# A gated cross-attention and ternary FFN block on one core: gate factor apart, last down product in column halves, weight rounding on GpSimd without the wait on VectorE

## What is computed

```python
qp = ctx @ Wq.T + bq;  kp = ctx @ Wk.T + bk
scores = (qp @ kp.T) * 128 ** -0.5 * layernorm(x)      # 512 x 512 for each of 4 batches
p = softmax(where(mask, -inf, scores))
x = x + tanh(g_xattn) * p

def quant_weight(w):                                   # ternary weights
    scale = mean(abs(w)) + EPS
    return clip(round(w / scale), -1, 1), scale
def quant_act(x):                                      # 8-bit rows
    s = max(abs(x), axis=-1) / 127 + EPS
    return clip(round(x / s), -128, 127), s
def qlinear(x, w): wq, ws = quant_weight(w); xq, xs = quant_act(x); return xq @ wq.T * xs * ws

h = layernorm(x)
x = x + tanh(g_ffn) * qlinear(silu(qlinear(h, w_gate)) * qlinear(h, w_up), w_down)
```

## Time and profile before

| | us |
|---|---|
| median of 3 runs | 224.27 (223.83 to 224.95) |
| the profiled execution | 224.45 |
| its span in the trace | 222.5 |
| TensorE busy in the span | 199.3 |
| VectorE busy | 180.2 |
| ScalarE busy | 124.5 |
| GpSimd busy | 97.8 |

### The profile page before, as it was taken

The page is one execution under the profiler, slowest core; times in us unless marked ns, Lnnn a source line. Parts: engine busy times, 40 slices in busy tenths (PEclk is TensorE's granted clock), DMA queues, the critical chain, the costliest instruction groups (busy, mean ns, idle before and its releaser), DMA issues.

```text
span 222.5 us, 2846 instructions
## 1 busy us (share of the span) xinstructions
PE 199.3 (90%) x854; PEld 90.3 (41%) x854; DVE 180.2 (81%) x359; ACT 124.5 (56%) x165; POOL 97.8 (44%) x154
## 2 busy tenths in 40 slices
PE   8764008999999998999999999999999999999994
PEld 7221004344444344444444444444444444444441
DVE  0598979799989799797997989888898987888721
...
PEclk9995555899999999999999999999999999999999
...
GB/s 215 420 423 423 417 391 424 281 325 8 3 47 47 115 186 172 98 0 3 47 64 121 153 91 15 69 80 74 141 3 175 201 89 13 96 79 16 97 188 94
DMA packets 47360, 32.84 MB, mean 148 GB/s; under 512 B 40944, under 2 KB 41072, under 8 KB 45808
## 3 DMA queue, kind: packets, MB, share of 16 engines
...
## 4 chain that ended last, share of the span: by engine, by line
PE 71%; DMA 14%; ACT 5%; DVE 4%; issue 2%; SPq 2%; DVEq 0%
PE pU L947 23%; PE pG L934 23%; PE pD L965 20%; DMA stage_b<-in_L_ffn_w_up 8%; DMA stage_a<-in_L_ffn_w_down 4%; PE pA L909 3%; ACT down_w L689 2%; DMA stage_b<-stage_b 2%; ACT L736 1%; ACT hid L736 1%; DVE abs_part L1345 1%; SPq L351 1%; PE pA L898 1%; ACT stage_b L743 1%; DVE am L1320 1%
## 5 line engine op out<-in xcount | busy, mean ns | idle before, releaser
L736 ACT ACTIVATE hid<-pG,act_g 128x512 f32<-128x512 f32 x64 | 43.6, 688 | 54.6 <-PE pG L934 54.4
L934 PE MATMUL pG<-gate_w,xqT 128*128 128x512 f16 x256 | 64.7, 388 | 1.4 <-DVE xqT L1303 0.8
L947 PE MATMUL pU<-up_w,xqT 128*128 128x512 f16 x256 | 62.7, 379 | 0.0
L965 PE MATMUL pD<-down_w,stage_b 128*128 128x512 f16 x256 | 57.3, 379 | 0.6 <-DMA stage_b<-stage_b 0.6
L1311 DVE TENSOR_TENSOR hid<-pU,hid 128x512 f32<-128x512 f32 x64 | 43.6, 685 | 11.1 <-PE pU L947 9.2
L934 PEld LDWEIGHTS pG<-gate_w,xqT 128*128 128x128 f16 x256 | 25.1, 100 | 37.0 <-issue 8.0
L965 PEld LDWEIGHTS pD<-down_w,stage_b 128*128 128x128 f16 x256 | 24.9, 98 | 31.8 <-issue 2.3
L947 PEld LDWEIGHTS pU<-up_w,xqT 128*128 128x128 f16 x256 | 25.1, 98 | 31.3 <-issue 1.7
L743 ACT ACTIVATE stage_b<-hid,inv 128x1024 f16<-128x1024 f32 x15 | 16.9, 1139 | 7.8 <-DVE inv L1329 7.8
L560 POOL TENSOR_SCALAR out_scale<-den,act_e,down_k 128x1 f32<-128x1 f32 x16 | 5.9, 371 | 33.4 <-DVE den L1326 33.4
L909 PE MATMUL pA<-kT,qT 128*128 128x512 f32 x26 | 15.4, 678 | 4.9 <-ACT kT L709 4.9
...
## 6 DMA issues: line engine op xcount, KB each, us to landing
...
out<-x SPq DMA_DIRECT2D x8, 256.0 KB, 2.4
out<-stage_b SPq DMA_DIRECT2D x8, 256.0 KB, 2.4
ctx_s<-in_ctx SPq DMA_DIRECT2D x4, 256.0 KB, 14.4
...
```

The lines of the kernel that those rows point to most:

```text
L736: act.activation(hid[:, t % NH, n * 512:(n + 1) * 512], pG[c % NG][:, :], ACT.Silu, scale=act_g[:, t:t + 1]).then_inc(silu_done, 1)
L934: ins = pe.matmul(pG[c % NG][:, :], xqT[:, t // TILES % 2, t % TILES, k, :], gate_w[:, n, k, :], start=k == 0, stop=k == KD - 1)
L947: ins = pe.matmul(pU[c % NU][:, :], xqT[:, t // TILES % 2, t % TILES, k, :], up_w[:, n, k, :], start=k == 0, stop=k == KD - 1)
L965: ins = pe.matmul(pD[t % ND][:, :], hidT[:, t % 2, k, :], down_w[:, k // KD, k % KD, :], start=k == 0, stop=k == KI - 1)
```

## The change

Four things, and a new order of all engines' lists around them.

- The factor `rsum * tanh_g` becomes one VectorE instruction per group of tiles (`rgate[:, t0:t1]`). Where GpSimd adds the residual, the multiplication of `probs` by it is a call of its own, `gate_probs(t)`, on ScalarE (9 tiles: 4, 6 to 10, 12, 14, 15) or GpSimd (1, 5, 13). VectorE still does tiles 0, 2, 3 and 11 in one instruction.
- The down product of tile 15 is made in column halves: 16 matmuls of 256 columns into one `pD` bank, then 16 into the other, with a `residual2_columns` and a `store_columns` of 128 KB for each.
- GpSimd's `weight_round` no longer waits for the bound of the chunk ahead.
- `k_copy(1)` and `k_copy(2)` go to VectorE. In the tables `CENTRE_BY`, `QUANTISE_BY`, `HQ_BY`, `ABS_BY` and `SIGN_BY` other engines are named. Each of the five lists is in another order.

```diff
+        GATE_BY = "-P--APAAAAA-APAA"
-        ABS_BY = ["AAAV", "AVAA", "AAAA"]
-        SIGN_BY = ["QXXX", "QQQX", "XXQQ"]
+        ABS_BY = ["AAVA", "AAAA", "AAAA"]
+        SIGN_BY = ["XQXQ", "QQXQ", "QXQX"]
...
             def residual1(t):
-                probs_t = probs[:, t % NP, :]
-                pool.wait_ge(tanh_done, 1)
-                pool.wait_ge(rsum_done, group_of(t) + 1)
-                pool.tensor_scalar(probs_t, probs_t, rsum[:, t:t + 1], tanh_g[:, 0:1], ALU.mult, ALU.mult)\
-                    .then_inc(gated, 1)
-                pool.wait_ge(gated, upto(RESIDUAL_BY, t))
-                pool.tensor_tensor(xt(t), probs_t, xt(t), ALU.add).then_inc(x2_pool, 1)
+                who = GATE_BY[t]
+                pool.wait_ge({"A": gated_act, "P": gated_pool}[who], upto(GATE_BY, t))
+                pool.tensor_tensor(xt(t), probs[:, t % NP, :], xt(t), ALU.add).then_inc(x2_pool, 1)
...
                 pool.wait_ge(winv_done, m + 1)
-                if m or n:
-
-                    wait_ternary(pool, *divmod(NC * m + n - 1, NC))
...
+            def gate_probs(t):
+                probs_t = probs[:, t % NP, :]
+                act.wait_ge(rgate_ready, group_of(t) + 1)
+                act.activation(probs_t, probs_t, ACT.Identity, scale=rgate[:, t:t + 1]).then_inc(gated_act, 1)
...
+            def down_columns(t, half):
+
+                cols = slice(half * 256, half * 256 + 256)
+
+                bank = pD[(t + half) % ND]
+                pe.wait_ge(final_ready, t - ND + 1 + half)
+                for k in range(KI):
+                    if half == 0 and k % 8 == 0:
+                        pe.wait_ge(hidT_ready[t % 2][k // 8], 16 * (t // 2 + 1))
+                    ins = pe.matmul(bank[:, cols], hidT[:, t % 2, k, :], down_w[:, k // KD, k % KD, cols],
+                                    start=k == 0, stop=k == KI - 1)
+                ins.then_inc(down_half, 1)
...
+            def residual2_columns(t, half):
+                cols = slice(half * 256, half * 256 + 256)
+                dve.wait_ge(down_half, 2 * t + half + 1)
+                if half == 0:
+                    dve.wait_ge(oscale_ready, t + 1)
+                dve.scalar_tensor_tensor(xt(t)[:, cols], pD[(t + half) % ND][:, cols], out_scale[:, t:t + 1], xt(t)[:, cols],
+                                         ALU.mult, ALU.add).then_inc(final_ready, 1)
```

More of the change, by code:

```diff
@@ L584, in _ @@
             valid_sums(0)
+            exp_bias(1)
             mask(2)
[L586 removed]
+            gate_probs(1)
             residual1(1)
[L588 removed]
             valid_sums(1)
[L590 removed]
+            centre(0)
             std2(0)
+            gate_scales(0)
             quantise_x(0)
[L593 to L597 removed]
+            centre(2)
             std2(1)
[L599 to L600 removed]
+            weight_round(0, 1)
             quantise_x(2)
@@ L815, in _ @@
             silu(6, 0)
+            silu(6, 1)
+            quantise_hidden(4, 0)
+            silu(6, 2)
+            quantise_hidden(4, 1)
+            silu(6, 3)
+            silu(7, 0)
             exp(8)
@@ L819, in _ @@
             exp(11)
-            silu(6, 1)
-            quantise_hidden(4, 1)
-            silu(6, 2)
-            silu(6, 3)
             quantise_hidden(5, 1)
-            silu(7, 0)
             silu(7, 1)
-            centre(8)
+            gate_probs(8)
+            gate_probs(9)
+            gate_probs(10)
             quantise_hidden(6, 0)
+            quantise_hidden(6, 1)
+            centre(9)
             silu(7, 2)
@@ L1135, in _ @@
             gate(10, 3)
+            gate(11, 0)
             up(10, 3)
-            gate(11, 0)
             up(11, 0)
@@ L1464, in _ @@
+            product(3, 0)
+            absmax_hidden(2, 1)
+            weight_bound(2, 3)
+            absmax_x(4)
+            inverse_hidden(2)
+            stats2(5)
             product(3, 1)
-            inverse_hidden(2)
+            residual2(0)
             absmax_hidden(3, 0)
+            absmax_x(5)
             product(3, 2)
-            stats2(4)
+            inverse_x(2)
             product(3, 3)
-            residual2(0)
+            inverse_std2(2)
             absmax_hidden(3, 1)
-            absmax_x(4)
+            residual2(1)
@@ L1473, in _ @@
             inverse_hidden(3)
-            residual2(1)
-            stats2(5)
-            stats1(9)
             stats2(6)
-            absmax_x(5)
-            inverse_std2(2)
-            inverse_x(2)
+            reciprocal_scale(2)
+            stats2(7)
+            residual2(2)
             absmax_x(6)
-            residual2(2)
-            stats2(7)
+            inverse_std2(3)
+            absmax_x(7)
+            product(4, 0)
+            inverse_x(3)
+            product(4, 1)
             score(8)
-            reciprocal_scale(2)
@@ L1486, in _ @@
-            absmax_x(7)
+            absmax_hidden(4, 0)
             mask_and_max(8)
-            inverse_x(3)
+            residual2(3)
+            reciprocal_scale(3)
+            stats1(10)
             score(9)
-            residual2(3)
+            stats1(11)
             mask_and_max(9)
-            product(4, 0)
-            inverse_std2(3)
-            stats1(10)
-            product(4, 1)
+            stats1(12)
+            product(4, 2)
+            stats1(13)
+            product(4, 3)
@@ L1523, in _ @@
+            residual2(4)
+            product(6, 2)
+            gate_sums(3)
             product(6, 3)
+            absmax_hidden(6, 1)
+            product(7, 0)
+            inverse_hidden(6)
             stats2(8)
-            absmax_hidden(6, 1)
+            product(7, 1)
             stats2(9)
-            inverse_hidden(6)
-            residual2(4)
-            residual1(11)
             absmax_x(8)
-            product(7, 0)
+            residual2(5)
             absmax_x(9)
-            residual2(5)
@@ L1650, in _ @@
             residual2(14)
-            residual2(15)
+            residual2_columns(15, 0)
+            residual2_columns(15, 1)
 _TRANSPOSED = ("ctx_512", "L0_xattn_Wq", "L0_xattn_Wk", "L0_ffn_w_gate", "L0_ffn_w_up", "L0_ffn_w_down")
```

549 lines of the change are left out of this document (276 added, 273 removed).

## The result

The changed kernel takes **226.20 us** (median of 8 runs, 225.41 to 226.91), the kernel before 224.38 beside it: ratio **1.0078** (95%: 1.0065 to 1.0091), 1.8 us slower. The forecast of 223.5 and its sign were wrong; 226.2 is the last value of the range, and the case that came true is the second rival (226.0). The profiled execution took 226.07 us, its span is 224.3 us, against 224.45 and 222.5 before.

The account below looks back on a forecast made before the run. TensorE was taken as almost never idle from its first gate product, with VectorE and ScalarE having to keep up. 224.45 - 0.2 (front and middle) - 0.6 (end) = 223.65, or 223.5 against the 224.27 median; range 221.6 to 226.2.

Parts of the forecast that it names:

- the second rival: ScalarE's exponentials and table loads ahead of silu(1, 3) become the bound, 2.5 us more: 226.0; chance 0.22.
- What GpSimd gains by not waiting: GpSimd's weight_round without its wait: at most 4.8 us gained in one place, off TensorE's path, hidden.
- The walk through ScalarE's list: ScalarE's calls counted from 20.3 us with trace durations: last down chunk summed at 48.2, silu(1, 3) done at 62.7.
- TensorE's account: TensorE's work done by 62.7 us: new 22.9, old 23.8, so 0.9 behind; old then loses 1.3 us by 93.
- any slip of one engine: In ScalarE's exponential block before silu(1, 3), a slip passes to both other engines; 2.5 us more, 226.0; chance 0.22.
- Head start kept: Front: down chunks land 2.5 us apart, weight_sum(2) at 46.5, all behind it 1.7 us earlier: 221.8; chance 0.23.
- The end: Tile 15's column halves: 32 matmuls in 3.5 us, shorter residual and store; -0.6 us, bounds -0.8 and +0.9.
- The weight-load rival: Weight loads of the last down product's column halves show, 16 times 0.1 us: 225.1; chance 0.04.
- The gate factor: Behind 93 us, nine gate_probs on ScalarE, some 0.6 us each, lie beside down and up products.
- The signs of being wrong: Prediction wrong if TensorE has a new idle stretch behind 63 us, or the clock falls again between 35 and 48.

Follow-up runs that it names:

- a_old_wait: The changed kernel with GpSimd's old wait for the bound of the chunk ahead put back in weight_round: 224.72 us, ratio 1.0016.
- b_columns: The kernel before with only the last down product (tile 15) in column halves, two residuals and two stores: 223.68 us, ratio 0.9972.
- a_best: The changed kernel with GpSimd's old wait, silu(1, 3) before the exponentials, score(8) after up(2, 1), quantise_hidden(0, 0) and (0, 1) one call later: 222.91 us, ratio 0.9943.
- a_fixed_gate_pool: The changed kernel with GpSimd's old wait, silu(1, 3) before the exponentials, and nine gate_probs moved from ScalarE to GpSimd: 224.05 us, ratio 0.9979.
- a_old_silu13_again: Second measurement of the changed kernel with GpSimd's old wait and silu(1, 3) before the exponentials: 224.12 us, ratio 0.9978; the first gave 223.50 us, 0.9961.

## Why the prediction was wrong

**The sum, put together again.** The column halves alone: -0.28%, -0.6 us. The wait removed: +0.59% in the old order, +0.62% in the new one, +1.3 to +1.4 us. What is left is 0.78 + 0.28 - 0.62 = 0.44%, +1.0 us, for the new order with the gate factor apart (it is the difference of a_old_wait, 1.0016, and b_columns, 0.9972). The place of `silu(1, 3)` accounts for all of it: 1.1 to 1.2 us, in both orders of the two edits.

**The step that failed.** "What GpSimd gains by not waiting (4.8 us at most in one place, off TensorE's path) is hidden." I asked what the earlier rounding gains and not what it hits. The wait had a second effect: GpSimd's roundings could not start before VectorE's clip, so a clip and a rounding of GpSimd were never side by side; with it gone VectorE lost 4.3 us to such overlaps, with it back 0.6 (the mask of tile 7). The price of the edit is +1.4 us where I put nothing. The trace could have warned. Timeline of before, VectorE and GpSimd, rows that the prediction does not use:

```profile
41.77 0.68 DVE L1235 CUSTOM_DVE_ANT_0 probs<-probs,mask_u 128x512 f32<-128x512 f32 x1
42.02 2.27 POOL L553 TENSOR_SCALAR up_w<-stage_b,winv 128x2048 f16<-128x2048 f32 x1 [2.40 <-DVE up_w L1365]
...
56.78 1.97 POOL L553 TENSOR_SCALAR down_w<-stage_a,winv 128x2048 f16<-128x2048 f32 x1 [4.81 <-DVE down_w L1365]
58.72 1.27 POOL L468 TENSOR_TENSOR mask_u<-masks_u 128x512 int32<-128x512 int32 x1
...
59.47 1.07 DVE L1365 TENSOR_SCALAR down_w<-down_w 128x2048 f16<-128x2048 f16 x1
```

The 4.81 us are what I read as time that GpSimd wastes. But the rounding at 42.02 starts beside a mask and takes 2.27 instead of 1.97, and the clip at 59.47, beside GpSimd's `mask_u`, takes 1.07 instead of 0.68: it ends 0.55 us after that instruction.

**The walk through ScalarE's list.** It held well: first gate 31.2 forecast, 30.34 measured; the last down chunk's sum lets `weight_sum(2)` go at 48.2, measured 48.56; the exponentials end at 56.9, measured 57.2; ScalarE waits for the last two down chunks (1.28 and 1.46 us). It parts from the trace at the projections: the k copy came to an end at 62.6 where I had 60.8, and `silu(1, 3)` at 64.6 where I had 62.7. With the wait back it ends at 63.2, so 1.4 of these 1.9 us hang on the collisions; 0.5 I had simply counted short.

**TensorE's account.** "0.9 us behind there" was for 62.7. By the same working the 22.9 us of work were done at 64.65 instead, where the old kernel stands at 22.0 + 3.77 = 25.8: 2.9 behind. It loses 1.3 by 93 us, which leaves 1.6; measured at the last 64 down matmuls 2.06 (207.33 against 205.27). The 1.3 was too large: between 60.88 and 93.23 the old kernel's TensorE is busy 31.39 of 32.35 us, so it loses 0.96, which leaves 1.9. The method was right; its input was 1.9 us off and this term 0.3. So even without the collisions the forecast was too low: a_old_wait takes 224.7 and not 223.5, and its profiled execution lies 0.9 us above the sum, of which these 0.5 and 0.3 are 0.8.

**The rival that came true.** "ScalarE's block of exponentials becomes the bound", 226.0, "decides once `silu(1, 3)` ends behind 63.5". It ended at 64.6 and the time is 226.2. The place was right, and moving `silu(1, 3)` out of the block gives 1.1 us. What I called "any slip of one engine" had a cause that could be named, and that would have made this case the likeliest. That the number fits so well is in part luck. By the rival's own rule, a microsecond lost for each behind 63.5, an end at 64.6 would cost 1.1 us and not 2.7. The threshold is not borne out either: in a_old_wait `silu(1, 3)` ends at 63.2, in front of it, and the time is 224.7, 1.2 above the forecast.

**Head start kept** (221.8) fell: its condition was chunks landing 2.5 us apart, and ScalarE waited for them longer than I had counted. Only with the wait back and three places in ScalarE's and TensorE's lists mended (a_best, 222.9) does the early start bring anything beyond the column halves, 0.3%.

**The end** held in its parts but for one: 3.88 us for the 32 matmuls, 0.34 of it a wait for the second transposition ("0 to 0.9, I take 0"), 2.7 us from there to the span's end (2.6). With this wait the end is worth 0.3 us in the profiled execution (17.0 us from the last 64 down matmuls on, before 17.2) and not 0.6. The weight-load rival (225.1) is out: the loads take 0.10 us each in the profile's rows (90.3 us for 870) and lie beside matmuls.

**The gate factor** on ScalarE was put at nothing, in cover; a_fixed_gate_pool agrees.

**The signs of being wrong.** TensorE's late waits end at 62.65 (0.78 us) and 64.65 (0.88), and there is none behind. The second lies behind 63 us, which the prediction had named as a sign of being wrong ("a new idle stretch of TensorE stands behind 63 us"); it is the stall of `gate(2, 1)` that it had put at 62.7. The other sign, a clock that falls again in the gaps between 35 and 48, does not show in the profiled execution of after, and 7 of its 8 executions have 0.961 or 0.962. But the clock did fall there in a_old_silu13_again, for 3.4 us and at a cost of some 0.7, and the one execution of after with 0.955 was the slowest (226.91). The prediction had no term for this.
